# Fetching three of every 120 gathered columns row by row from SyncE, in a graph network of four layers

## The reference, cut to what matters

```python
# relation layer (h is the normed x)
hw = jnp.einsum('nd,rdf->rnf', features, weight_r)      # 8 relations
msg = hw[etype, src] / deg[dst][:, None]
M = jax.ops.segment_sum(msg, dst, num_segments=N)
# attention layer
e = jax.nn.leaky_relu(el[src] + er[dst], negative_slope=NEG_SLOPE)
m = jax.ops.segment_max(e, dst, num_segments=n)
ex = jnp.exp(e - m[dst])
den = jax.ops.segment_sum(ex, dst, num_segments=n)
msg = z[src] * (ex / den[dst])[:, None]
rst = jax.ops.segment_sum(msg, dst, num_segments=n)
```

## Time and profile before

| | us |
|---|---|
| median of 3 runs | 16974.48 (16973.96 to 16981.99) |
| profiled execution, from its first to its last instruction | 16976.7 |
| relation layer's block, about | 8488 to 12525 |
| attention layer's block, about | 12777 to 16835 |
| POOL busy | 12777.1 (75% of the span) |
| DVE busy | 8378.6 (49%) |
| ACT busy | 2611.6 (15%) |
| PE busy | 2069.2 (12%) |

### The profile page before, as it was taken

The page is one execution under the profiler, slowest core; times in us unless marked ns, Lnnn a source line. Parts: engine busy times, 40 slices in busy tenths (PEclk is TensorE's granted clock), DMA queues, the critical chain, the costliest instruction groups (busy, mean ns, idle before and its releaser), DMA issues. The chain is left out here.

```text
span 16976.7 us, 58414 instructions
## 1 busy us (share of the span) xinstructions
PE 2069.2 (12%) x17217; PEld 1932.5 (11%) x17217; DVE 8378.6 (49%) x5949; ACT 2611.6 (15%) x1261; POOL 12777.1 (75%) x13406
## 2 busy tenths in 40 slices
PE   1222333333333010110500000000000000000000
PEld 1212333333333010010300000000000000000000
DVE  7888988888887677777511111111131222222222
ACT  1000110101101223323311111111110101101101
POOL 7777777777777777777677777777777777777776
PEclk9997666666666555555755555555555555555555
DMA  4222211212121333333411221221232222222222
GB/s 79 55 54 68 69 66 64 69 60 69 60 69 58 103 109 116 113 107 117 130 49 50 54 54 50 54 54 50 54 46 46 55 51 55 55 51 55 55 51 55
DMA packets 611553, 1137.55 MB, mean 67 GB/s; under 512 B 329631, under 2 KB 381312, under 8 KB 569248
## 3 DMA queue, kind: packets, MB, share of 16 engines
q0 software_dynamic: 428736, 387.04, 12.2%
q10 hardware_dynamic: 33984, 425.89, 6.2%
q1 hardware_dynamic: 148512, 320.87, 5.9%
HBM read 613.19 MB, written 519.73 MB: 67 GB/s over the span
## 5 line engine op out<-in xcount | busy, mean ns | idle before, releaser
L946 POOL DMA_INDIRECT by_src<-H,sort_place_i x3224 | 3121.9, 968 | 983.5 <-issue 982.9
L465 POOL DMA_INDIRECT rel_G<-rel_table,rel_idx x3224 | 3045.7, 945 | 1013.5 <-issue 982.2
L465 POOL DMA_INDIRECT att_G<-att_table,att_idx x3224 | 3042.4, 944 | 982.5 <-issue 982.5
L465 POOL DMA_INDIRECT lead_rows<-h_table,wsum_idx x3044 | 2887.9, 949 | 927.6 <-issue 927.6
L656 DVE SCALAR_TENSOR_TENSOR rel_Gf<-rel_Sf,rel_keep_first,rel_Gf 128x64 f32<-128x64 f32 x55 | 18.5, 336 | 3517.5 <-ACT rel_Gf L787 3517.5
L630 DVE TENSOR_TENSOR_SCAN att_near<-att_near,er_in 128x60 f32<-128x60 f32 (+2 forms) x55 | 19.3, 352 | 2968.8 <-DMA att_G<-att_table,att_idx 2968.8
L1110 PE MATMUL pG<-sort_cnt,sort_lowT 128*128 128x98 f32 x6448 | 1116.1, 348 | 814.6 <-DVE sort_prod L1002 814.6
L1110 PEld LDWEIGHTS pG<-sort_cnt,sort_lowT 128*128 128x128 f32 x6448 | 1071.6, 261 | 822.7 <-DVE sort_prod L1002 822.7
L845 PE MATMUL wsum_C<-wsum_high,wsum_low 128*128 128x98 fp8e4 x6448 | 560.9, 282 | 3369.9 <-DVE wsum_high L510 3369.9
L845 PEld LDWEIGHTS wsum_C<-wsum_high,wsum_low 128*128 128x128 fp8e4 x6448 | 520.1, 142 | 3411.3 <-issue 3411.3
L509 DVE TENSOR_TENSOR wsum_low<-iota_b,wsum_parts 128x3840 fp8e4<-128x3840 bf16 x216 | 892.0, 4129 | 9.8 <-DVE wsum_parts L500 9.8
(11 more groups left out here) (366 smaller groups left out, 7620.8 us busy)
## 6 DMA issues: line engine op xcount, KB each, us to landing
scan_att<-att_S ACTq DMA_DIRECT2D x53, 1980.0 KB, 6.7
scan_wsum<-wsum_S ACTq DMA_DIRECT2D x53, 1920.0 KB, 6.5
sort_keys<-key_rows SPq DMA_DIRECT2D x53, 1920.0 KB, 9.6
scan_rel<-rel_S ACTq DMA_DIRECT2D x53, 1920.0 KB, 6.4
scan_pool<-pool_S ACTq DMA_DIRECT2D x70, 1440.0 KB, 5.2
pool_row<-by_src SPq DMA_DIRECT2D x35, 1485.0 KB, 6.0
by_src<-H,sort_place_i POOLq DMA_INDIRECT x3224
rel_G<-rel_table,rel_idx POOLq DMA_INDIRECT x3224, 2.4
```

What stands on the lines that cost most here:

```text
L465: pool.indirect_dma_start(out=G[s][:, j, :], out_offset=None, in_=table, in_offset=bass.IndirectOffsetOnAxis(ap=idx[s][:, j:j + 1], axis=0 ...
L946: pool.indirect_dma_start(out=by_src, out_offset=bass.IndirectOffsetOnAxis(ap=place_i[s][:, j:j + 1], axis=0), in_=row[s][:, j, :], in_off ...
```

## The change

`SINGLE = (2, 1)`: of each even chunk the last two columns, of each odd chunk the last column, are no longer fetched by POOL. This holds for chunks 0 to 52 (`FULL = 53`) of both layers; chunk 53 stays as it was. SyncE fetches them row by row. For a column these are 128 DMAs of one row (256 bytes, 260 in the attention layer) from the table in HBM to one partition of `G[s]`. The byte offset of the row in the table comes from a register; one instruction loads 16 such registers from a small tile in SBUF, then 16 DMAs use them.

```diff
@@ class SingleRows (new) @@
+            def vector(self, index):
+                by_chunk = index[:, 0:FULL * L].rearrange("p (k j) -> p j k", j=L)
+                for n in range(WIDEST):
+                    last = nc.vector.tensor_scalar(self.own[:, n, :], by_chunk[:, L - 1 - n, :], float(4 * self.width), None, ALU.mult)
+                last.then_inc(self.s_made, 1)
+            def move(self, sp):
+                sp.wait_ge(self.s_made, 1)
+                for n in range(WIDEST):
+                    sp.dma_start(self.dram[:, n * P:(n + 1) * P].rearrange("k p -> p k"), self.own[:, n, :],
+                                 allow_slow_non_contiguous=True).then_inc(self.s_moved, 16)
+                sp.wait_ge(self.s_moved, 16 * WIDEST)
+                sp.dma_start(self.ids[:], self.dram).then_inc(self.s_moved, 16)
+            def issue(self, sp, k, s, rows_of, table, landed):
+                wide = 4 * self.width
+                to = rows_of.rearrange("p j f -> p (j f)").bitcast(U8)
+                of = table.rearrange("n f -> (n f)").unsqueeze(0).bitcast(U8)
+                for n in range(SINGLE[s]):
+                    at = (L - 1 - n) * wide
+                    for p0 in range(0, P, BATCH):
+                        registers = [sp.alloc_register(f"{self.kind}_row{k}_{n}_{p0 + p}") for p in range(BATCH)]
+                        sp.load(registers, self.ids[k:k + 1, n * P + p0:n * P + p0 + BATCH])
+                        for p, register in enumerate(registers):
+                            place = sp.snap(register, donate=True, min_val=0, max_val=4 * self.width * (self.places - 1))
+                            sp.dma_start(to[p0 + p:p0 + p + 1, at:at + wide], of[:, bass.ds(place, wide)]).then_inc(landed[n][k % 4], 16)
@@ gathered_layer @@
+                def await_rows(engine, i, s, w=L):
+                    engine.wait_ge(gathered[s], grouped(i, s, w))
+                    if w == L:
+                        for n in range(ALONE[s]):
+                            k = 2 * i + s
+                            engine.wait_ge(alone[n][k % 4], 16 * P * (k // 4 + 1))
@@ sync @@
+                    if single:
+                        for k in range(FULL):
+                            sp.wait_ge(turned, k + 1)
+                            single.issue(sp, k, k % 2, G[k % 2][:], table, alone)
@@ gpsimd @@
-                        for j in range(w):
+                        for j in range(in_groups(s, w)):
@@ vector own, scalar own @@
-                            dve.wait_ge(gathered[s], 16 * L * i + 16 * w)
+                            if kind != "rel":
+                                await_rows(dve, i, s, w)
-                                act.wait_ge(gathered[s], 16 * L * i + 16 * w)
+                                await_rows(act, i, s, w)
@@ first_layers, and alike relation_update @@
+                    single.move(sp)
...
+                    single.await_moved(sp)
...
+                    single.vector(rel_idx)
```

More of the change, by code:

```diff
@@ L63, in build @@
     FM = D + 2
+    SINGLE = (2, 1)
+    WIDEST = max(SINGLE)
+    FULL = NCH - 1
+    BATCH = 16
     assert NCH % 6 == 0 and HT % TG == 0 and L % WAYS == 0 and NP > N and NP < 2 ** 15 and WAYS == 2 * BANKED and BANKED * HT <= 512
@@ L81, in build @@
     low_last = nc.dram_tensor("low_last", [P, LAST], U8, kind="Internal").ap()
+    single_ids = {kind: nc.dram_tensor(f"single_ids_{kind}", [FULL, WIDEST * P], I32, kind="Internal").ap() for kind in ("rel", "att")}
     ctx = ExitStack()
@@ L305, in _, with __init__, scratch, await_moved @@
                 sp.wait_ge(s_table, 16 * (10 + NPC))
+        class SingleRows:
+            def __init__(self, kind, width, c, places):
+                self.kind, self.width, self.places = kind, width, places
+                self.ids = sb(f"{kind}_single_ids", [FULL, WIDEST * P], I32, c)
+                self.dram = single_ids[kind]
+            def scratch(self, c):
+                self.own = sb(f"{self.kind}_single_own", [P, WIDEST, FULL], I32, c)
+                self.s_made, self.s_moved = (semaphore(f"{self.kind}_single_{n}", c) for n in ("made", "moved"))
+            def vector(self, index):
[10 more added lines that the diff above has]
+                sp.dma_start(self.ids[:], self.dram).then_inc(self.s_moved, 16)
+            def await_moved(self, sp):
+                sp.wait_ge(self.s_moved, 16 * WIDEST + 16)
+            def issue(self, sp, k, s, rows_of, table, landed):
[10 more added lines that the diff above has]
+                            sp.dma_start(to[p0 + p:p0 + p + 1, at:at + wide], of[:, bass.ds(place, wide)]).then_inc(landed[n][k % 4], 16)
@@ L310, in gathered_layer @@
         def gathered_layer(kind, table, width, rows_out, c0, c1, index, counts=None, pooled=False, weights=None,
-                           carried=None, key_first=None, spread=None):
+                           carried=None, key_first=None, spread=None, single=None):
             F = FM if kind == "att" else D
@@ L327, in gathered_layer @@
             BY, PBY = 512 // L, 512 // SIDE
+            ALONE = SINGLE if single else (0, 0)
+            in_groups = lambda s, w: w - (ALONE[s] if w == L else 0)
+            grouped = lambda i, s, w=L: 16 * (L - ALONE[s]) * i + 16 * in_groups(s, w)
             with ExitStack() as c:
@@ L350, in gathered_layer @@
                 stored = [sem(f"stored{s}") for s in range(2)]
+                alone = [[sem(f"alone{n}_{q}") for q in range(4)] for n in range(max(ALONE))]
+                def await_rows(engine, i, s, w=L):
[4 more added lines that the diff above has]
+                            engine.wait_ge(alone[n][k % 4], 16 * P * (k // 4 + 1))
                 same_ready, scanned, issuing = sem("same_ready"), sem("scanned"), sem("issuing")
@@ L764, in number_following @@
                     def number_following(i, s):
-                        act.wait_ge(gathered[s], 16 * L * i + 16 * L)
+                        act.wait_ge(gathered[s], grouped(i, s))
                         if REST and s == 0 and type(i) is int and i == NC // 2 - 1:
@@ L1371, in add_taken, with first_layers @@
                                     in_=taken[:, 0:D], in_offset=None, compute_op=ALU.add).then_inc(landed, 16)
-        def first_layers():
+        def first_layers(single):
             with ExitStack() as c:
+                single.scratch(c)
                 V, VP = sb("V_wsum", [P, HT, D], c=c), H
@@ L1483, in _ @@
                     v.memset(rel_idx[:, J:], 0)
-                    v.scalar_tensor_tensor(rel_idx[:, 0:J], src_all[:, 0:J], float(R), rel_idx[:, 0:J], ALU.mult, ALU.add)
+                    st.done(v.scalar_tensor_tensor(rel_idx[:, 0:J], src_all[:, 0:J], float(R), rel_idx[:, 0:J], ALU.mult, ALU.add))
+                    single.vector(rel_idx)
                     for s in range(2):
@@ L1632, in _, with relation_update @@
                             turn_pairs(tiles(H, n - 2), 512).then_inc(s_hturned, 1)
-        def relation_update(er, at_i, key_first, spread):
+        def relation_update(er, at_i, key_first, spread, single):
             with ExitStack() as c:
+                single.scratch(c)
                 V = sb("V_rel", [P, HT, D], c=c)
@@ L1678, in _ @@
                     v.tensor_copy(key_first[:], dst_all[:, 1:2])
+                    single.vector(src_all)
                     st = Steps(dve, s_steps)
@@ L1812, in build @@
             rel_idx = sb("rel_idx", [P, JP + 2 * L], I32, c)
-            first_layers()
-            gathered_layer("rel", rel_table, D, scan_rel, 0, NCH, rel_idx)
+            rel_single = SingleRows("rel", D, c, R * NP)
+            first_layers(rel_single)
+            gathered_layer("rel", rel_table, D, scan_rel, 0, NCH, rel_idx, single=rel_single)
         er, at_i, key_first = sb("er_nodes", [P, HT]), sb("at_i", [P, HT], I32), sb("key_first", [P, 1], I32)
         spread = semaphore("er_spread")
-        relation_update(er, at_i, key_first, spread)
-        gathered_layer("att", att_table, D + 1, scan_att, 0, NCH, src_all, key_first=key_first, spread=spread)
+        att_single = SingleRows("att", D + 1, ctx, NP)
+        relation_update(er, at_i, key_first, spread, att_single)
+        gathered_layer("att", att_table, D + 1, scan_att, 0, NCH, src_all, key_first=key_first, spread=spread, single=att_single)
         attention_update()
```

## The result

| | before | after |
|---|---|---|
| median of 4 runs each, us | 16977.24 (16973.96 to 16981.99) | 17806.56 (17793.98 to 17813.69) |
| profiled execution, us | 16976.7 | 17812.0 |
| ratio, with its 95% interval | | 1.0488 [1.0473, 1.0503] |

Forecast were 16,778 us and a gain. The time came out 1,029 us above that, above the upper end of the range too.

The account below looks back on a forecast made before the run. POOL's column fetches were taken to bound both layers. Removing 80 columns a layer saves 199.8 us, less 3 us of setup, 197 us: 16,974.5 becomes 16,778 us, with SyncE's work hidden; range 16,755 to 17,080 us.

Parts of the forecast that it names:

- POOL bounds both layers: In both layers a chunk takes what POOL needs for its columns, 1.2493 and 1.2484 us each.
- 80 columns: Columns leaving POOL in each layer, worth 99.9 us a layer, 199.8 us together.
- The landing and the waits: A chunk's rows are waited for at its end, so only the last one's landing counts; costed at nothing.
- the setup: Two small DVE instructions and two DMAs in each block ahead of the layers; mostly hidden, 3 us put in `first_layers`.
- keep pace over the layer: SyncE need not keep pace within a chunk, only on the whole, with about one chunk of lag allowed.
- The test: SyncE's sum a layer, forecast 3,502 us, against POOL's 3,873 (hidden) and 3,973 us (no gain).
- d: Price of one DMA of one row on SyncE: taken 0.287 us, bounds 0.27 and 0.48.
- l: Price of one SyncE load of 16 registers from SBUF: taken 0.88 us, 563 us for 640 loads.
- what was to show its failure: POOL's waits name ACT or DVE, which wait for a SyncE DMA at a chunk's end; period over 75 us.
- rival 2: On SyncE, a DMA with a register in its address is dearer, deciding from 0.333 us; 17,730 us at 0.37; chance 0.08.
- rival 1: On SyncE, the load of registers is the bound at 1.8 to 2.0 us each; 17,210 to 17,470 us; chance 0.12.

Follow-up runs that it names:

- e2b_fixed_rows: Changed kernel with its 10,240 one-row DMAs a layer at fixed addresses and no register loads: 16,798.33 us, 0.9881 of the kernel before.
- e7_setup_only: Changed kernel with only the setup in the two blocks ahead, POOL fetching all columns: 19,771.29 us at the slower pace, 0.9996 of the kernel before.
- e8b_pattern67: Changed kernel with two columns of every fourth chunk and one of the others on SyncE, 67 a layer: 16,826.77 us, 0.9904 of the kernel before.
- e4b_small_store: Changed kernel with ScalarE storing 4 of each chunk's 60 columns in the relation layer alone: 17,631.90 us, 1.0377 of the kernel before.
- e1_one_one: Changed kernel with one column of every chunk on SyncE, 53 a layer: 22,803.86 us at the slower pace, 1.153 of the kernel before.
- e2_fixed_rows: Changed kernel with all one-row DMAs at fixed addresses and no register loads: 22,801.76 us at the slower pace, 1.1526 of the kernel before.
- e3_one_load: Changed kernel with one load of 16 registers for each column in place of eight: 24,452.86 us at the slower pace, 1.2361 of the kernel before.

## Why the prediction was wrong

**Right.** POOL bounds both layers, at 1.25 us for a column, and 80 columns are worth 99.9 us a layer: e2b_fixed_rows has the gain. The landing and the waits cost nothing that shows, the setup neither (e7_setup_only, 10 us at the most), where 3 us were put. SyncE has to keep pace over the layer, not in each chunk (e8b_pattern67). The test was the right one, 10,240 x d + 640 x l against 3,873 and 3,973, and what was to show its failure is what the waits of the profile after show.

**The step that failed** is the price of a DMA, d = 0.287. "A register in the address is not to be seen anywhere in the trace" was followed by a value from rows of the same shape but with fixed addresses, and rival 2 was put down with "the address is one more operand of an instruction that already costs 0.287". The register brings an instruction of its own, and the fixed-address DMA too was dearer than taken. A row costs, from start to start:

```
                          taken   e2b_fixed_rows   the changed kernel
the DMA, not held         0.287       0.298             0.271
held beside stores          -         0.017             0.017
its MOVE                    -           -               0.061
together                  0.287       0.315             0.349
```

0.349 is inside the bounds of 0.27 to 0.48, and above the 0.323 and 0.333 from which the sum decides. Of the 638 us that it adds to a layer, 0.034 a row or 348 us are the register (the MOVE, less what the DMA itself is shorter), 178 are the stores, and 112 are left for a pitch that three rows at the start gave a little low. By d alone, with the load at its 0.88, the sum is 3,577 + 563 = 4,140 us, 167 over 3,973, and the kernel slower.

**The term that was mis-sized** is l: 1.288 in place of 0.88 us, 261 us a layer. By itself it lies under the break-even of 1.46, and with d as taken the kernel would still have gained (2,939 + 824 = 3,763). But it took up the margin for d: with l = 1.288 a row may cost (3,873 - 824) / 10,240 = 0.298 us before SyncE decides. The bounds were fair, the value was built from VectorE's shortest read and a gap for each register; the per-register part, 0.045, was close to the measured 0.057, the fixed part, 0.16, was half of the measured 0.34. The row behind that 0.16 (L614, 128x1) reads one number in each partition, not 64 bytes of one as rival 1's counter-argument has it.

**None of the parts decides by itself.** The sum was off by 4,401 - 3,502 = 899 us a layer: 348 of the register, 178 beside the stores, 112 of the pitch, 261 of the loads. With the 348 alone it would be 3,850 us, 23 under POOL's 3,873 and still hidden; the 178 on top make 4,028, over 3,973. Without the 348 the other three make 4,053, slower as well. These are sums of measured terms, not runs.

Of the two pages that spoke to l, neither gives it. "DMA: Bandwidth & Descriptors" of the Trainium skill, section "Latency and other measured facts", has a floor of about 600 ns: 8 registers take 792 ns here, which does not contradict it, but 16 take 1,255, and it says nothing of the growth by register. "Runtime: NRT & Kernel Launch" of the Trainium skill, section "Instruction fetch mechanics", has about 200 ns for each register, for what the page describes as loads of registers from HBM; the runs, which load from SBUF, have 57. The measurements decide.

**What rival it was.** The place is that of rival 2, and its condition, d over 0.333, is met at 0.349; its time of 17,730 at 0.37 was worked out with the cheaper load (0.37 is also not half way between 0.287 and 0.48; that is 0.384, and the time would be 18,010). With both measured terms its own arithmetic gives 16,974.5 + 2 x 428 = 17,830 us, 0.1% above the measured 17,806.6. It had a chance of 0.08, and all that speaks against it was an argument about operands. A chance of 0.68 for the forecast was too high for a sum with a margin of 10% and two prices that no row showed: both had the same sign of risk, and each was taken in the lower half of its bounds.

**Not tried** was a layer in which another engine's queue does part of the issuing, and a load from elsewhere than SBUF.

## What to carry to other kernels

Work out what a unit is worth where it leaves and what it costs where it goes: here a column of 128 rows gives POOL 1.25 us back and takes SyncE 128 x 0.349 + 8 x 1.288 = 55 us, so the idle queue can take one column in 45, at most 70 of the 3,180 of the 53 chunks; 67 gained 1%, 80 lost 5%. Past the even point each column costs 55 us, not 1.25, so stay below it when a price is unknown. Before pricing an operand that no row shows, look in the trace of a small kernel for the instructions that it brings: the list of SyncE's instructions that stood ahead of the prediction goes from DMA to DMA and has no MOVE. In a sum over 10,000 of them one of 29 ns used up nearly the whole margin of 371 us.

## What the runs showed of the hardware

- A DMA whose address holds a register is issued as MOVE and DMA on SyncE: the MOVE 29 ns, with its gap 0.061 us from start to start. The DMA itself is a little shorter, 228 ns against 252 with a fixed address (medians), so the pair costs 0.034 us more.
- A load of registers out of SBUF on SyncE: 0.34 us and 0.057 for each register (0.79, 1.25 and 2.16 us for 8, 16 and 32; a straight line through medians).
- SyncE's issue of a DMA of one row lasts, in the changed kernel, up to 1.16 us just behind a store of 1.9 MB on ScalarE's queue, and some 178 us are lost in a layer of 53 such stores; with the stores cut to a fifteenth no DMA is over 332 ns (e4b_small_store). Why is not shown; POOL's indirect DMAs, 944 ns, were not slower beside SyncE's 20,000 instructions.
- At the held pace some of SyncE's short instructions take about 1.4 us from start to start, MOVEs and DMAs alike: 1,073 of the 6,784 MOVEs and 1,125 of the DMAs in the relation layer of e1_one_one take over 1.2 us. Their durations there:

```profile
L361 SPq MOVE rel_G<-rel_table x6784: 1/29/1411, 10299.4 to 16309.5; - x200
L361 SPq DMA_DIRECT2D rel_G<-rel_table x6784: 1/228/1421, 10299.5 to 16309.5; - x200
```

  The median is the usual one, the longest MOVE 1,411 ns in place of 42. The relation layer's gather of e7_setup_only:

```profile
L535 POOL DMA_INDIRECT rel_G<-rel_table,rel_idx x3224 | 3474.2, 1078 | 1137.6 <-issue 1012.4 <-ACT rel_idx L813 125.3
```

  1,078 ns in place of 945 for an indirect DMA, but this with SyncE idle; in e1_one_one, e2_fixed_rows and e3_one_load, where SyncE bounds, POOL's keep 943 to 945 ns. The kernels in which SyncE issues thousands of DMAs lose most there: 80 columns cost 24% (e3_one_load) where they otherwise gain 1%. The cause of the held pace was not found.
